# Four blocks of tokens between two expert layers: another order of the work of two neighbouring blocks, and one Pool operation instead of two for a reciprocal root

## The reference, cut to what matters

```python
x = x + _L0_attn_ref(_layernorm(x), ...)      # eight heads over 2048 tokens
x = x + _L0_ffn_ref(_layernorm(x), ...)       # 64 experts, the best 6 of a token, and a shared one
x = x + _L1_attn_ref(_layernorm(x), ...)      # the lookup, below
x = x + _L1_ffn_ref(_layernorm(x), ...)       # 8 experts, the best 2 of a token
...
def _L1_attn_ref(x, W_off, b_off, W_attn, b_attn, W_out, b_out):
    off = (x @ W_off + b_off).reshape(Bx, Nx, H, P, 2)
    w = jax.nn.softmax((x @ W_attn + b_attn).reshape(Bx, Nx, H, P), axis=-1)
    idx = off[..., 0].astype(jnp.int32)
    ...
    x0 = x[:, 0, :]
    g = jnp.take_along_axis(x0, idx.reshape(Bx, -1), axis=1).reshape(Bx, Nx, H, P)
    s = jnp.sum(g * w, axis=(2, 3))
    out = jnp.broadcast_to(s[..., None], (Bx, Nx, C))
    return out @ W_out + b_out
```

## Time and profile before

| what | value |
|---|---|
| median of 3 runs | 1053.69 us (1052.11 to 1057.41) |
| profiled execution | 1054.79 us, of which the span of the core is 1053.0 us |
| busy in the span | PE 71%, DVE 66%, ACT 42%, Pool 37% |
| granted TensorE clock, mean | 0.841 |
| attention of layer 0 | about 0 to 456 us |
| routing and experts of layer 0 | 456 to 703 us |
| gathers, lookup, routing of layer 1 | 703 to 922 us |
| experts of layer 1, output | 922 to 1053 us |

### The profile page before, as it was taken

How to read it: one execution, slowest core, us unless ns; L and a number is a source line. 1 busy time by engine, 2 the same in 40 slices (tenths; PEclk the granted TensorE clock), 3 DMA queues, 4 the chain that set the end, 5 groups by cost and what they waited for, 6 DMA issues and landing times.

```text
span 1053.0 us, 18639 instructions
## 1 busy us (share of the span) xinstructions
PE 744.9 (71%) x5996; PEld 431.5 (41%) x5996; DVE 691.4 (66%) x1389; ACT 442.8 (42%) x570; POOL 393.6 (37%) x505
## 2 busy tenths in 40 slices
PE   3533699989998998945757778850456365199992
PEld 2201222322232232222547777740233242199992
DVE  5688899999999999936335554323665754334442
ACT  1350388867876876830213333320100101155550
POOL 5000000024423621646423333337765733635553
PEclk9855699999999999976979999985565566589997
DMA  4999999999991100151464444422111101123335
GB/s 134 279 279 279 279 339 334 283 282 288 286 301 38 44 4 7 44 133 37 154 234 120 121 121 123 133 79 53 48 52 41 49 30 40 49 38 46 53 51 135
DMA packets 79485, 143.17 MB, mean 136 GB/s; under 512 B 10320, under 2 KB 73136, under 8 KB 77632
## 3 DMA queue, kind: packets, MB, share of 16 engines
q1 hardware_dynamic: 55088, 119.33, 38.7%
q0 software_dynamic: 12784, 17.40, 7.4%
q10 hardware_dynamic: 11520, 5.25, 1.9%
HBM read 116.76 MB, written 101.34 MB: 207 GB/s over the span
## 4 chain that ended last, share of the span: by engine, by line
PE 52%; DVE 23%; POOL 8%; issue 7%; DMA 4%; ACT 3%; SPq 1%; POOLq 1%; DVEq 0%
PE PS L518 10%; PE PS L825 6%; PE PS L503 6%; PE PS L493 6%; PE PS L653 5%; DVE PS L1319 4%; PE PS L655 3%; PE PS L835 3%; POOL GB L1110 3%; DVE XQ L1395 3%; POOL slots_scratch L1076 2%; DVE small L1244 2%; DVE hm L1227 2%; DMA XP<-slots_scratch 2%; PE PS L641 2%
## 5 line engine op out<-in xcount | busy, mean ns | idle before, releaser
L903 ACT ACTIVATE PB<-PS 128x1024 f32<-128x1024 f32 x256 | 262.1, 1025 | 116.9 <-PE PS L503 107.7
L1319 DVE TENSOR_SCALAR PS<-PS 128x1024 f32<-128x1024 f32 x256 | 301.6, 1227 | 11.3 <-PE PS L493 7.8
L518 PE MATMUL PS<-PB,VS 128*32 128x256 f32 x2048 | 165.6, 396 | 0.6 <-ACT PB L903 0.6
L1076 POOL DMA_INDIRECT slots_scratch<-XN,slot x96 | 93.7, 976 | 59.8 <-ACT PB L903 38.7
L503 PE MATMUL PS<-QM,KP 64*128 64x512 bf16 x512 | 101.4, 393 | 14.4 <-DVE PS L1319 14.3
L1097 POOL COPY WQ<-W0GU 128x192 f32 x160 | 60.1, 376 | 125.6 <-PE PS L655 97.4
L1110 POOL DMA_INDIRECT GB<-y_scratch,slotc x96 | 91.7, 955 | 36.3 <-issue 28.6
L493 PE MATMUL PS<-QS,KP 64*128 64x512 bf16 x512 | 100.6, 390 | 5.3 <-DVE QM L1261 2.9
L1395 DVE COPY XQ<-PS 128x256 f32<-128x256 f32 x80 | 34.0, 425 | 97.7 <-PE PS L641 97.7
L1085 POOL TENSOR_TENSOR X<-X,TQ 128x256 f32<-128x256 f32 x8 | 5.8, 725 | 220.1 <-DVE TQ L1270 220.1
L653 PE MATMUL PS<-XQ,WQ 128*96 128x128 f32 x320 | 65.9, 288 | 30.6 <-DVE XQ L1395 23.1
(11 more groups left out here) (264 smaller groups left out, 1222.2 us busy)
## 6 DMA issues: line engine op xcount, KB each, us to landing
y_scratch<-YP SPq DMA_DIRECT2D x80, 128.0 KB, 1.8
slots_scratch<-slots_scratch SPq DMA_DIRECT2D x1, 8768.0 KB, 32.6
W0GU<-in_w0gu SPq DMA_DIRECT2D x1, 6144.0 KB, 51.9
XP<-slots_scratch ACTq DMA_DIRECT2D x80, 64.0 KB, 2.1
XP<-slots_scratch SPq DMA_DIRECT2D x80, 64.0 KB, 1.9
W1GU<-in_w1gu SPq DMA_DIRECT2D x1, 4096.0 KB, 13.1
W0D<-in_w0d SPq DMA_DIRECT2D x1, 3072.0 KB, 16.7
XG<-slots_scratch SPq DMA_DIRECT2D x39, 68.5 KB, 2.0
```

The costliest lines, as they stand in the source:

```text
L518: last = mm(PS[32 * j:32 * j + 32, at + q.start:at + q.stop], VS[:, n, g * HG + j, :], PB[u // 2 % 3][:, 2 * (j % 2) + j // 2, q], start=( ...
L903: A(PB[u // 2 % 3][:, 2 * hp:2 * hp + 2, :], pair_banks(u).rearrange("p (j q) -> p j q", j=2), ACT.Exp).then_inc(sem("exp_done"), 1)
L1076: gp.indirect_dma_start(slots0_dram.rearrange("b p d -> (b p) d"), bass.IndirectOffsetOnAxis(ap=slot0[:, t, k:k + 1], axis=0), XN[:, t, 0: ...
L1319: TS_(pair_banks(u), pair_banks(u), 4.0, 0.0, ALU.mult, ALU.max).then_inc(sem("relu_done"), 1)
```

## The change

On DVE, PE and ACT the loop over blocks gets another order. Turn q now holds the first half of block q's lookup (norm, offsets, indices, the transposes of the indices) and the second half of block q-1's (fills, products, `lookup`, `looked_up`, its layer 3 norm and routing). `fills` and `filled` are cut in two parts that can stand apart. The last turn holds, behind that, the second half of block 3 as well. A table, `TURN`, numbers the eight transposed blocks in their new order, and waits are set accordingly. Pool puts the power of layer 2 behind 5 gathers of the next block and the power of layer 3 behind 22; of the dispatches the first now stands ahead of the layer 3 power of block 2. The routing's logits and counts move from bank 7 to bank 1. In `lookup` four products for the output bias become one of 512 columns. The sum of six gathered rows stays as it was.

Besides, at all norms, the addition of epsilon goes from Pool to DVE, behind the aggregation, with a wait of its own; Pool does the power alone.

```diff
+        TURN = {(2, 0): 0, (2, 1): 1, (3, 0): 2, (2, 2): 3, (3, 1): 4, (2, 3): 5, (3, 2): 6, (3, 3): 7}
...
             for q in range(NC):
+                chunk_turned(2, q, 0)
                 if q >= 1:
-                    chunk_turned(2 * q - 1, "xn3_ready", q - 1, 2)
-                chunk_turned(2 * q, "xn2_ready", q, 0)
-                if q >= 1:
-                    router1(q - 1)
+                    fills(q - 1, 0)
                 offsets(q)
                 if q == 0:
                     tables()
                 else:
+                    fills(q - 1, 1)
+                weights_turned(q)
+                if q >= 1:
+                    lookup(q - 1)
+                if q == NC - 1:
+                    fills(q, 0)
+                if q >= 1:
+                    chunk_turned(3, q - 1, 2)
+                if q == NC - 1:
+                    fills(q, 1)
+                if q >= 1:
+                    router1(q - 1)
+                if q == NC - 1:
+                    lookup(q)
+                if q >= 1:
                     counts1(q - 1)
-                weights_turned(q)
-                fills(q)
-                lookup(q)
-            chunk_turned(2 * NC - 1, "xn3_ready", NC - 1, 2)
+            chunk_turned(3, NC - 1, 2)
...
             for q in range(1, NC):
-                gathers(q, 0, TOP0)
+                gathers(q, 0, 5)
+                chunk_scale(2, q - 1)
+                gathers(q, 5, 22)
                 if q >= 2:
-                    chunk_scale(2 * q - 3, "moments3", q - 2)
-                chunk_scale(2 * q - 2, "moments2", q - 1)
-                gathers(q, TOP0, 4 * TOP0)
-            chunk_scale(2 * NC - 3, "moments3", NC - 2)
-            chunk_scale(2 * NC - 2, "moments2", NC - 1)
+                    chunk_scale(3, q - 2)
+                gathers(q, 22, 4 * TOP0)
+            chunk_scale(2, NC - 1)
             pool.wait_ge(sem("padded"), 48)
             chunk_dispatch(0)
+            chunk_scale(3, NC - 2)
             chunk_dispatch(1)
-            chunk_scale(2 * NC - 1, "moments3", NC - 1)
+            chunk_scale(3, NC - 1)
             chunk_dispatch(2)
             chunk_dispatch(3)
...
-                for t in range(4 * q, 4 * q + 4):
-                    last = v.bn_aggr(moments[:, t, :], stats[:, t, :])
-                last.then_inc(sem(name), 1)
...
+                for i in range(4 * q, 4 * q + 4):
+                    last = v.bn_aggr(moments[:, i, :], stats[:, i, :])
+                step(last)
+                TS_(moments[:, t, 1], moments[:, t, 1], EPS, None, ALU.add).then_inc(sem(name), 1)
...
-            scaled(2 * NC - 1, NC - 1, "xn3_ready")
-            router1_logits(NC - 1)
-            router1_chosen(NC - 1)
-            router1_slots(NC - 1)
+            q = NC - 1
+            scaled(2, q)
+            filled(q - 1, 0)
+            lookup_index(q)
+            filled(q - 1, 1)
+            looked_up(q - 1)
+            moments_of(q - 1, "moments3")
+            filled(q, 0)
+            scaled(3, q - 1)
+            filled(q, 1)
+            router1_logits(q - 1)
+            looked_up(q)
+            moments_of(q, "moments3")
+            router1_chosen(q - 1)
+            scaled(3, q)
+            router1_slots(q - 1)
+            router1_logits(q)
+            router1_chosen(q)
+            router1_slots(q)
```

More of the change, by code:

```diff
@@ L749, in _, with fills @@
             FILLS = [("b", 0), ("w", 0), ("b", 1), ("b", 2), ("w", 1), ("b", 3), ("a", 0), ("a", 1), ("r", 0), ("r", 1)]
-            def fills(q):
+            def fills(q, part):
                 x = slice(q * CH, (q + 1) * CH)
                 pe.wait_ge(sem("ti_ready"), 2 * q + 2)
-                d = 8 * q
-                for kind, i in FILLS:
+                d = 8 * q + 4 * part
+                for kind, i in FILLS[6 * part:6 + 4 * part]:
                     if kind == "w":
@@ L1278, in chunk_stats @@
                 step(last)
-                for t in range(4 * q, 4 * q + 4):
-                    last = v.bn_aggr(moments[:, t, :], stats[:, t, :])
-                last.then_inc(sem("moments_chunk"), 1)
+                t = slice(4 * q, 4 * q + 4)
+                for i in range(4 * q, 4 * q + 4):
+                    last = v.bn_aggr(moments[:, i, :], stats[:, i, :])
+                step(last)
+                TS_(moments[:, t, 1], moments[:, t, 1], EPS, None, ALU.add).then_inc(sem("moments_chunk"), 1)
             def chunk_scores(q):
@@ L1506, in lookup_tables, with filled @@
                 last.then_inc(sem("tables_ready"), 1)
-            def filled(q):
-                for d in range(8):
+            def filled(q, part):
+                for d in range(4 * part, 4 * part + 4):
                     n = 8 * q + d
```

138 lines of the change are left out of this document (73 added, 65 removed).

## The result

| what | before | after |
|---|---|---|
| median | 1053.87 us (1052.11 to 1057.41, 4 runs) | 1065.82 us (1064.13 to 1066.88, 4 runs) |
| profiled execution, span | 1054.79, 1053.0 | 1066.17, 1064.3 |
| granted clock, mean | 0.841 | 0.836 |

The changed kernel is slower: 1.0108 times before, with a 95% interval of 1.0078 to 1.0137. The forecast was 1064.4 us.

The account below looks back on a forecast made before the run. A round of short answers between engines bounds the kernel. Last power +7.8, transfers behind it +2.6, attention epsilon +0.4, first norm -0.1 make +10.7 us on 1054.79, 1065.5; the median is 1.1 lower: 1064.4 us, range 1054 to 1071.

Parts of the forecast that it names:

- What bounds the kernel: Block turns between 703 and 922 us: a round of short answers between engines, with neither Pool nor DVE full.
- The walk: Middle turn followed step by step from T, the end of layer 2's power: 43.0 us, against 42.6 and 39.9 before.
- PE's stand: Ahead of the second table pair, PE waits for the bank `AW` frees, from about T+11 to T+17.7.
- three signs of being wrong: Pool's wait behind 22 gathers under 2 us, turns under 38 us, or a tail under 40.
- The lookup: PE's lookup products in a middle turn: 4.9 us, with the one-product bias form taking the same time as before.
- The table pair: Second pair of table products in a middle turn: 3.0 us, between 3.8 at low clock and 2.1 at high.
- The tail: Last turn, with two second halves in it: 45.5 us against 34.65 before, a loss of 10.9 us.
- Behind the last power: First dispatch of block 2 waits for slots that DVE does after the last normed rows: 2.6 us more.
- The start: Up to the first gather: epsilon on DVE costs 0.4 us in the attention and saves 0.1 in the first norm.
- Pool's pace: Rival, chance 0.08: Pool's gathers set turns of 32.4 us, total 10.5 us faster, 1043.
- The high clock: Rival, chance 0.20: PE's clock high throughout, turns 41.2 us, tail 43, +4.6 us, about 1058; counted as no change.
- The low clock: Rival, chance 0.06: table pairs 3.8 us and lookups 7.5, turns about 45.5, tail 53, total 1077.

Follow-up runs that it names:

- the kernel with `AW` early: Changed kernel with `AW` and its fills ahead of the indices and `PR` straight behind them: 1051.83 us, ratio 0.9964 to the kernel before.
- The kernel with the power alone: Kernel before with only the epsilon addition moved to DVE and one power on Pool: 1054.96 us, ratio 1.0000.
- the kernels with short sums: Changed kernel and kernel before, each with one multiply-add of six per weighted sum: ratios 0.9678 and 0.9880 on the second chip, 0.9718 and 0.9914 on the third.

## Why the prediction was right, and which terms were off

**What bounds the kernel** was read rightly. The turn is a round of answers between engines; Pool's waits and DVE's load are not what sets it. Moving one early operation that PE waits for gave 4.1 and 6.7 us in the two whole turns, on the usual chip. Taking 7.6 us of DVE's work out of a turn gave 3 to 5, and moving Pool's power gave nothing that shows; both of these ran on other chips.

**The walk** held step by step in the first whole turn. T is the end of the power at 772.08, 773.1:

| step | predicted | first turn |
|---|---|---|
| first fill | T+2.4 | T+2.3 |
| `AW` starts | T+17.0 | T+16.9 |
| second table pair done | T+20.7 | T+21.4 |
| addition of the lookup starts | T+26.8 | T+25.0 |
| layer 3 aggregation and epsilon done | T+29.0 | T+27.2 |
| router's answer on DVE | T+34.2 | T+33.4 |
| end of the next power | T+43.0 | T+41.7 |

PE's stand ended where I had it, at T+17.7, but it began at T+13.7 and not at T+11, because the first pair came later and ran at the low clock. None of the three signs of being wrong appeared: Pool's wait was 6.05 and 8.51 us, both whole turns were over 38 us and the tail over 40.

**The sizes that were off** are these.
- *The lookup.* I took 4.9 us and no change of form. It took 3.1 us in the first turn (794.88 to 797.98), mostly beside a sum, and about 5.5 in the second, at the low clock. The step that failed is "the same columns, so the same time": nine products took 3.10 us where twelve with as many columns took 4.29, both at a clock of 1.00, and the diff shows an earlier wait that I passed over. In the old order the new lookup, with both, is worth 10 us, and I had put it at 0.
- *The table pair.* I took the middle, 3.0. It was 3.7 in the first turn (790.84 to 794.52) and 3.8 in the second. The Trainium skill, in "TensorE: Matmul & The Clock Gate", section "Part 1: The HAM clock gate", has the throttled state as the default, and by that rule these pairs would be at the low clock; the rows agree. The granted clock was 0.50 in the pair ahead of the stand and 0.53 in the pair behind it, so the stand did not lower it. Without the stand it rose in the midst of the pairs, as the kernel with `AW` early shows (1.00 in its second pair), and behind the short stand of the last turn, 1.27 us, the pair took 2.0 us at 1.00.
- The two cancel in part: the turns were 41.7 and 44.5, in sum 86.2 where I had 86.0.
- *The tail.* 45.5 predicted, 42.1 measured. Two lookups in it ran at the high clock and cost 3.1 each instead of the 4.3 at which I had priced them, 2.4 us in all. The three table pairs were no gain: 7.7 us (874.30 to 876.29, 887.81 to 890.73 and 891.38 to 894.21) against 6.3. The rest is in small terms, as the router's products with 0.95 us and not 1.7.
- *Behind the last power.* 2.6 us more predicted, 4.2 measured. The first transfer starts 4.88 us behind the power's start, before 1.23: DVE's slots came 0.6 us later than I had them. And the second transfer again lost time, 1.36 us where before it lost 0.74, for which I had no loss at all in the new order.
- *The start.* The first gather is 0.95 us later (704.64 against 703.69); I had 0.3 for attention and the first norm. The kernel with the power alone had its first power 1.7 us later than before and the same total, so I can't tell this from what two runs differ by.
- *The end.* The last sum on Pool is 9.9 us later than before and the end of the span 11.3. The 1.4 us between are in the last transfers, and I had no term for them.

The sum: the last power ends 5.4 us later (901.40 against 895.99). Of these 0.95 are the later start, for which I had 0.3 as a term of its own, and 4.5 are turns and tail, where I had 7.8. The transfers behind it add 4.2 and not 2.6, the rest up to the end 1.7 and not 0. The total of +11.3 against +10.7 is closer than its parts deserve: turns and tail were 3.3 us too dear, the rest 3.9 us too cheap, and that they cancel is luck.

**The rivals.** Pool's pace was refuted by the turns (41.7 and 44.5 us, where it asked for 32.4), and the kernels with short sums did not reach it either (39.1 to 41.0). The high clock came true in part of the tail. The low clock came true for the table pairs of both turns and for one lookup. The sign on another chip is something that no rival had.

## What to carry to other kernels

Before two blocks are interleaved, ask of each step who waits for it, and issue first what frees a bank or a buffer for another engine, even if it is short: one pair of DVE operations behind the wrong neighbour, with the fills that go with it, cost 14 us here. Read the waits in a diff as closely as the instructions; a wait that was split in two was part of a step worth 10 us that looked like a mere change of form. Before you explain what a change of one step is worth, look at the clock in that step on both sides: here one lookup at the low clock, on either side of the comparison, made most of the difference between 3.5 and 9.7 us. And time small changes of order on more than one chip, since near relatives of these two kernels came out in the other sequence on two others.

## What the runs showed of the hardware that I had not expected

- With equal columns, twelve products of 128 columns took 4.29 us and one of 512 with eight of 128 took 3.10, both at a granted clock of 1.00.
- On two of three chips the same kernel took 1131 and 1132 us where it took 1057 on the first, with small DVE operations spaced at 1.40 us instead of 0.2 to 0.4 in parts of the program, for which the profile names no other engine of the core. A good part of the loss, 22.6 us in one of them, lies in a stretch without such gaps.
- The same code in the same place ran a turn at a granted clock of 0.63 on one of these chips and at 0.50 on the other, 39.2 against 41.0 us.
